# Reordering the last stage of a two-layer convolution kernel: expansions in threes, and evictions by halves of both images

## What is computed

```python
r = relu(batchnorm(x @ Wr + br))                 # 64 -> 16 channels
w = (r @ Ws + bs)                                # 16 -> 16 groups x 9 taps
xi = x @ Wi + bi                                 # 64 -> 64 channels
patches = nine shifts of xi (zero padded), regrouped to [16, 4, 9]
out = sum over taps of w * patches
x = x + out
```

## Time and profile before

| | |
|---|---|
| median of 3 runs | 664.91 us (664.14 to 664.97) |
| the profiled execution | 664.74 us, its span 663.0 us |
| PE busy | 628.3 us, 95% of the span |
| DVE busy | 521.5 us, 79% |
| ACT busy | 326.9 us, 49% |
| POOL busy | 180.9 us, 27% |
| last stage | from about 444 us to the end |

### The profile page before, as it was taken

How to read it: one execution, slowest core, us unless ns; L and a number is a source line. 1 busy time by engine, 2 the same in 40 slices (tenths; PEclk the granted TensorE clock), 3 DMA queues, 4 the chain that set the end, 5 groups by cost and what they waited for, 6 DMA issues and landing times. The chain is left out here.

```text
span 663.0 us, 15413 instructions
## 1 busy us (share of the span) xinstructions
PE 628.3 (95%) x5984; PEld 250.4 (38%) x5984; DVE 521.5 (79%) x816; ACT 326.9 (49%) x451; POOL 180.9 (27%) x193
## 2 busy tenths in 40 slices
PE   6869899899999999999999999989999999999995
PEld 6433333333333333333333323323444444444442
DVE  5689875998666776667687899949988888898885
ACT  3645532311432142224213656744787787787761
POOL 2100240006400720081018003512352243244230
PEclk9879999999999999999999999997999999999998
DMA  8930030032323243225312633000121312222132
GB/s 318 226 72 1 1 86 1 1 91 78 97 72 97 73 103 91 71 72 141 99 29 70 165 93 92 1 9 8 41 50 41 72 42 48 60 54 48 44 69 64
DMA packets 67461, 47.95 MB, mean 72 GB/s; under 512 B 53602, under 2 KB 54596, under 8 KB 67396
## 3 DMA queue, kind: packets, MB, share of 16 engines
q1 hardware_dynamic: 67108, 46.82, 28.5%
q10 hardware_dynamic: 288, 0.21, 0.1%
HBM read 35.15 MB, written 9.76 MB: 68 GB/s over the span
## 5 line engine op out<-in xcount | busy, mean ns | idle before, releaser
L758 PE MATMUL conv<-xpad,comb 64*64 64x512 f32 x2016 | 227.4, 596 | 4.4 <-DVE x L1385 4.2
L1648 DVE TENSOR_TENSOR x<-conv,x 128x512 f32<-128x512 f32 x288 | 177.9, 682 | 24.4 <-PE conv L813 23.1
L758 PEld LDWEIGHTS conv<-xpad,comb 64*64 64x64 f32 x2016 | 75.0, 134 | 136.6 <-issue 121.5
L813 PE MATMUL conv<-rstack,wse 98*128 98x512 f32 x288 | 95.7, 438 | 1.7 <-DVE xin L1431 0.9
L829 PE MATMUL att<-x,cmp 64*32 64x512 f32 x1280 | 80.6, 602 | 0.0
L813 PEld LDWEIGHTS conv<-rstack,wse 98*128 98x128 f32 x288 | 48.5, 190 | 70.7 <-DVE x L1648 64.0
L1317 DVE SCALAR_TENSOR_TENSOR xpad<-att,x 128x1024 f32<-128x1024 f32 x46 | 54.1, 1219 | 23.6 <-PE att L608 23.3
L959 ACT ACTIVATE x<-conv,bias 128x512 f32<-128x512 f32 x40 | 25.3, 683 | 90.9 <-PE conv L758 90.8
L1800 POOL TENSOR_TENSOR x<-x,xin 128x1024 f32<-128x1024 f32 x15 | 36.0, 2397 | 111.6 <-ACT x L1111 111.6
L950 ACT ACTIVATE comb<-experts,small 128x768 f32<-128x768 f32 (+1 forms) x33 | 27.4, 859 | 75.6 <-PE conv L727 45.4
L1727 POOL TENSOR_TENSOR rt<-rt 128x16 f32<-128x16 f32 x12 | 5.1, 423 | 196.5 <-ACT rt L922 195.8
(11 more groups left out here) (212 smaller groups left out, 755.9 us busy)
## 6 DMA issues: line engine op xcount, KB each, us to landing
experts<-forms SPq DMA_DIRECT2D x72, 192.0 KB, 3.9
experts<-forms SPq DMA_DIRECT2D x72, 144.0 KB, 2.9
x<-in_x SPq DMA_DIRECT2D x32, 256.0 KB, 5.5
out<-comb SPq DMA_DIRECT2D x30, 256.0 KB, 3.3
rstack<-rstack SPq DMA_DIRECT2D x16, 128.0 KB, 2.3
experts<-in_We SPq DMA_DIRECT2D x1, 1152.0 KB
forms<-experts SPq DMA_DIRECT2D x2, 576.0 KB, 5.7
out<-comb SPq DMA_DIRECT2D x4, 128.0 KB, 2.2
```

Of the source, the lines that this page charges most:

```text
L758: last = nc.tensor.matmul(conv[own[to], h, HW * rows:HW * rows + HW], comb[own[rows], q % 2, n, tap(t)], xpad[own[rows], 2 * (q % 2) + n, ...
L813: nc.tensor.matmul(conv[:, unit, cols], wse[:, ORDER[i], :], rstk[s][0:RR, cols], start=True, stop=True).then_inc(exp_full, 1)
L1648: v.tensor_tensor(img(prod[i])[:, rows, :], img(conv[:, unit, :])[:, rows, :], xip[s][:, kh + 16 * h:kh + 16 * h + 16, kw:kw + W], ALU.mul ...
```

## The change

PE's order in a steady pair becomes

`E0 E1 | P (k+1) | E2 | A3 A4 (k-1) | E3 E4 E5 | XI (k+1) | A0 | E6 E7 | TB (k-1) | E8 | A1 A2`

ACT's becomes `empty_r`(k+1), sums of k-1, `empty_xi`(k+1), normalise(k+2), `empty_pix`(k-1), and POOL's the low part of k+1, then the residual of k-1. `sum_of` puts half h of both images into bank h, so that half 0 of both images lies in one bank on 128 partitions, in the right order; it is evicted in one instruction of 128x512. Half 1 still takes two. The evictions of the sums and of XI so have three instructions in place of four each. ACT's first and last pairs outside the loop are more, since the normalising runs two pairs ahead.

```diff
-PARTS_OF_SUM = 4
+PARTS_OF_SUM = 3
...
             first = 64 * (n ^ h)
-            return slice(first, first + 64), slice(n * HW, (n + 1) * HW)
+            return slice(first, first + 64), slice(h * HW, (h + 1) * HW)
...
                 expand(k, s, 1)
+                if not last:
+                    project(k + 1, 1 - s, m)
+                expand(k, s, 2)
                 if not first:
                     add_up(k - 1, 3)
                     add_up(k - 1, 4)
-                expand(k, s, 2)
-                expand(k, s, 3)
-                if not last:
-                    project(k + 1, 1 - s, m)
-                expand(k, s, 4)
-                expand(k, s, 5)
-                add_up(k, 0)
+                for i in (3, 4, 5):
+                    expand(k, s, i)
                 if not last:
                     project_xi(k + 1, 1 - s, m + 1)
+                add_up(k, 0)
                 expand(k, s, 6)
                 expand(k, s, 7)
+                if not first:
+                    turn_back(k - 1, m if last else m + 2)
+                expand(k, s, 8)
                 add_up(k, 1)
                 add_up(k, 2)
-                expand(k, s, 8)
-                if not first:
-                    turn_back(k - 1, m if last else m + 2)
...
             def empty_xi(s, m):
                 eng.wait_ge(misc_full, m + 1)
+                nc.scalar.activation(xip[s][:, 1:17, 1:W + 1], img(att[:, 1, :])[:, 0:16, :], ACT.Identity, bias=bi_s[:, 0:1])
                 for n in range(2):
-                    for h in range(2):
-                        rows, bank = sum_of(n, h)
-                        done = nc.scalar.activation(
-                            xip[s][own[n], 1 + 16 * h:17 + 16 * h, 1:W + 1],
-                            att[rows, 1, bank].rearrange("p (a b) -> p a b", b=W), ACT.Identity, bias=bi_s[rows, 0:1])
+                    rows, bank = sum_of(n, 1)
+                    done = nc.scalar.activation(
+                        xip[s][own[n], 17:33, 1:W + 1],
+                        att[rows, 1, bank].rearrange("p (a b) -> p a b", b=W), ACT.Identity, bias=bi_s[rows, 0:1])
                 done.then_inc(misc_free, 1)
...
                 eng.wait_ge(sum_done, len(ROUNDS) * (k + 1))
+                nc.scalar.activation(fin[:, 0:HW], att[:, 0, 0:HW], ACT.Copy).then_inc(sum_emptied, 1)
                 for n in range(2):
-                    for h, cols in halves():
-                        rows, bank = sum_of(n, h)
-                        nc.scalar.activation(fin[64 * n:64 * n + 64, cols], att[rows, 0, bank], ACT.Copy)\
-                            .then_inc(sum_emptied, 1)
+                    rows, bank = sum_of(n, 1)
+                    nc.scalar.activation(fin[own[n], HW:S], att[rows, 0, bank], ACT.Copy).then_inc(sum_emptied, 1)
...
             def involve(k, s, first=False, last=False):
                 m = 2 if first else 3 * k + 2
                 if not last:
-                    normalise2(k + 1, 1 - s)
+                    empty_r(k + 1, 1 - s, m)
                 if not first:
                     empty_sum(k - 1)
                 if not last:
-                    empty_r(k + 1, 1 - s, m)
                     empty_xi(1 - s, m + 1)
+                if not (isinstance(k, int) and k >= NP - 2):
+                    normalise2(k + 2, s)
                 if not first:
                     empty_pix(k - 1, 1 - s, m if last else m + 2)
...
+            normalise2(1, 1)
             involve(0, 0, first=True)
-            involve(1, 1)
-            involve(2, 0)
+            for k in range(1, 5):
+                involve(k, k % 2)
             eng.wait_ge(nmr_ready, 6)
-            with eng.Fori(1, GP - 1) as i:
+            with eng.Fori(2, GP - 2) as i:
                 involve(2 * i + 1, 1)
                 involve(2 * i + 2, 0)
-            involve(NP - 1, 1, last=True)
+            for k in range(NP - 3, NP):
+                involve(k, k % 2, last=(k == NP - 1))
...
             def involve(k, s, first=False, last=False):
+                if not last:
+                    r_lo(k + 1, 1 - s)
                 if not first:
                     finish(k - 1)
-                if not last:
-                    r_lo(k + 1, 1 - s)
...
             inverse_root(5, slice(GP, NP), GP)
+            eng.wait_ge(nmr_ready, 6)
```

## The result

The changed kernel takes 680.9 us (median of four executions, 678.9 to 682.49), the kernel before 664.75; the ratio is 1.0243, with a 95% interval of 1.0208 to 1.0278. It is slower. Two of the four executions took 679.5 and 678.9, two 682.3 and 682.5, and the profiled one is among the latter; timed again (e8) the kernel took 679.52 us, ratio 1.0224 (1.0210 to 1.0238), with nothing near 682. In the two profiles the spans differ by 17.7 us, of which 3.03 lie ahead of the last stage. So the change costs about 14.7 us; the 3 us are followed up in e6 to e8.

The account below looks back on a forecast made before the run. PE was taken as the bound, busy all 12.755 us of a pair. Pairs rise to 13.74, 0.985 each, 13.8 for pairs 1 to 14, plus 0.6 for the first: 664.74 + 14.4 = 679.1, stated as 679.0; range 669 to 685.

Parts of the forecast that it names:

- PE's blocks as units, and the old order without slack: Last stage, PE: busy throughout a 12.755 us pair, about 0.23 of it one wait; the new pair is summed block by block.
- E3 E4 E5: PE's three expansions in a row: E5's second half waits for DVE's product 3, 2.30 us in place of 1.68 without wait.
- TB's wait: PE at TB: it must wait for ACT to evict XI, whose misc half it writes; 0.50 us a pair.
- POOL hides, with 0.2 to spare: POOL: low part from about 5.4 after E0, residual done at 10.2, before TB starts at about 10.4.
- A pair 13.74 predicted: Steady pair of the last stage: blocks sum to 13.24 us, TB's wait makes 13.74, which is 0.985 over 12.755.
- The first pair: First pair of the last stage: no TB, statistics slow DVE; costs 0.6 us, between 0 and 1.
- pair 1: First of pairs 1 to 14, each taken to cost a steady pair's 0.985 us, together 13.8.
- the last: Last pair of the last stage: two groups of six halves, 4.6 us against 4.7 before; cost 0, give or take 0.4.
- TB not waiting: Rival at TB: E5 waits but TB does not, as ACT is quicker or E6 and E7 later; 672 us, chance 0.12.
- Faster: Rival at E3 to E5 and XI: DVE and evictions in time, a pair 12.61 us; 662.7 us, chance 0.06.
- Taking turns at a bank: Rival at sums and XI: row groups sharing a bank take turns, six blocks a pair double; about 756 us, chance 0.05.

Follow-up runs that it names:

- e8: The changed kernel run again without an edit, against the kernel before: 679.52 us, ratio 1.0224.
- e6: The changed kernel with a wait putting POOL's two instructions on the expanded weights behind DVE's row differences, against the kernel before: 679.34 us, ratio 1.0217.
- e4: The changed kernel with A1 moved behind A0 and XI moved between E4 and E5, against the kernel before: 667.58 us, ratio 1.0043.
- e3: The changed kernel with A1 moved right behind A0, between XI and TB, against the kernel before: 673.36 us, ratio 1.0133.
- e5: The changed kernel with POOL's old order, residual ahead of the low part, against the kernel before: 679.34 us, ratio 1.0221.
- e2: The changed kernel's orders with the four old evictions of XI and of the sums and the old banks, against the kernel before: 689.78 us, ratio 1.0376.
- e1: The kernel before with only the change's banks and three evictions each for sums and XI, no order changed: 665.01 us, ratio 1.0003.
- e7: The kernel before with a wait putting POOL's two instructions on the expanded weights behind DVE's row differences, against the kernel before: 664.73 us, ratio 1.0001.

## Why the prediction was right

It said 679.0 us and slower with 0.90; the kernel took 680.9 in the first four executions and 679.5 in e8, where the profile shows DVE ahead of POOL.

- **PE's blocks as units, and the old order without slack.** Nine of eleven blocks came within 0.02 of the sum's terms, their places changed or not.
- **E3 E4 E5: 2.30 predicted, 2.32 measured,** DVE named by both of E5's loads. e4 takes the wait away by what stands between E4 and E5 alone.
- **TB's wait: 0.50 predicted; E6 E7 grew by 0.40.** The term was a little too long: ACT began 1.20 after XI and three evictions took 2.08, as in the working, but PE followed ACT's end by 0.05, not 0.15. On the other hand TB to E8 took 0.92 where 0.81 was assumed. The two errors cancel, which is luck; e3, where both go, gains 0.52 there and 0.47 a pair.
- **POOL hides, with 0.2 to spare:** 0.22 in the profile, and e5 shows that giving it 0.8 more changes nothing. Its low part began 5.1 after E0 (574.46 to 579.54), not 5.4: the 1.54 taken from P to its eviction was read from a pair in which ACT was still evicting sums until 581.31.
- **A pair 13.74 predicted, 13.77 measured.** Thirteen pairs gave 13.2 us. The first pair cost 1.1 where 0.6 was taken (16.29 against 15.23 in the profiles, 16.32 in e8), pair 1 only 0.3 where 0.985 was taken (14.18 against 13.88), the last with the end 0.1 (23.6 against 23.5): together 14.7, against 14.4. The misses at the first pair and at pair 1 nearly cancel, which is luck too; they are read from the pairs' lengths, and why was not tried. The rest of the profiled run, 3.0, goes with the collision ahead of the last stage.
- **The rivals.** TB not waiting: e2 answers it, 0.7 more eviction is 0.7 more pair. Faster: DVE's start after an expansion did not shrink, it is 0.54 still (579.15 to 579.69). Taking turns at a bank: e1 finds no cost. The rule of the Trainium skill (TensorEngine Tiling (Array Packing), Restrictions and Gotchas), that different row tiles cannot access one PSUM bank at the same time, is what would have brought about the rival's 756 us. Here both row groups write each bank, on disjoint partitions, and A0 takes 0.88 in e1 where it took 0.89 with a bank for each. The measurement decides.

## What to carry to other kernels

With two buffers between a producer and a consumer, longer runs of the producer don't feed the consumer better: the third item of a run waits for the first to be consumed, start-up included, so count what stands between item i and item i + 2, not how long the run is. An eviction that costs nothing in one order can set the pace in another: before moving a block up, find whose buffer it reuses and count the work left between. Saving instructions on an engine that nobody waits for gives nothing by itself (e1), and the eviction of XI in that same saving is worth its full 0.70 a pair once a wait hangs on it (e2).

## What the runs showed of the hardware

**A wait costs more than itself.** When TB had to wait, its first weight load started with the release, not under the matmuls ahead of it: the eight transposes then took 0.91 to 0.92 to the next block, against 0.80 to 0.81 without a wait (e3, e4). In the changed kernel the first load and the first transpose both start at 584.80; in e3 the loads start at 565.57 and the transposes at 565.80.

**DVE and POOL take whole turns.** Who starts 0.06 us earlier goes first, and the other's instruction is longer by the rest of it: DVE 3.72 in place of 1.28 beside a POOL instruction of 2.63. The Trainium skill (SBUF — State Buffer, SBUF: two separate sides) describes this as an exclusive lock on a port pair that a GpSimd instruction and a DVE instruction with two SBUF inputs share, held for the whole instruction; the rows agree with it. A race that close is settled differently from execution to execution (POOL was 0.06 ahead in the first profile of the changed kernel, DVE 0.07 in e8), and can look like an effect of a change made far away.
